# A decoder layer on one core: attention scores of a head on a 32-row tile, the router's columns beside the shared expert's, and a PE that is kept working ahead of the first product

## The reference

```python
# cross attention: 32 heads of 8 numbers, rotary positions on q and k
q = (x @ Wq).reshape(b, n, 32, 8);  k, v = split(ctx @ Wkv)
logits = einsum('bqhd,bkhd->bhqk', rope(q), rope(k)) / sqrt(8)
attn = einsum('bhqk,bkhd->bqhd', softmax(logits), v)
out = attn @ Wout + bout
# mixture of 8 experts (the best 2 by score), and a shared expert
scores = sigmoid(xt @ gate_w.T);  top_scores, sel = top_k(scores, 2)
h = silu(r @ w1[e].T) * (r @ w3[e].T);  out += h @ w2[e].T   # r = score * token
shared = silu(xt @ sw1.T) * (xt @ sw3.T) @ sw2.T
```

## Time and profile before

| | us |
|---|---|
| median of 3 runs | 674.62 (672.46 to 676.4) |
| profiled execution, its own time | 674.33 |
| its span in the trace | 672.4 |
| PE busy | 609.8 (91%) |
| DVE busy | 502.1 (75%) |
| ACT busy | 388.0 (58%) |
| POOL busy | 287.3 (43%) |

### The profile page before, as it was taken

How to read it: one execution, slowest core, us unless ns; L and a number is a source line. 1 busy time by engine, 2 the same in 40 slices (tenths; PEclk the granted TensorE clock), 3 DMA queues, 4 the chain that set the end, 5 groups by cost and what they waited for, 6 DMA issues and landing times. The chain is left out here.

```text
span 672.4 us, 14287 instructions
## 1 busy us (share of the span) xinstructions
PE 609.8 (91%) x4244; PEld 523.4 (78%) x4244; DVE 502.1 (75%) x1183; ACT 388.0 (58%) x1213; POOL 287.3 (43%) x326
## 2 busy tenths in 40 slices
PE   1887999999999999999999998646799999999998
PEld 1666888988888888888888888424578878878887
DVE  6884986987887888878869866824577867867756
ACT  2256557656756756665675666134576655656563
POOL 4353564654754754755646534356252112111000
PEclk9998999999999999999999999856989999999999
DMA  6000200200200200200202000161221211211100
GB/s 233 31 1 0 79 2 1 78 0 0 78 0 0 78 0 0 78 0 4 74 0 64 1 0 2 62 221 22 49 40 36 38 42 35 40 40 37 22 15 18
DMA packets 24142, 25.58 MB, mean 38 GB/s; under 512 B 3873, under 2 KB 19745, under 8 KB 23969
## 3 DMA queue, kind: packets, MB, share of 16 engines
q1 hardware_dynamic: 24096, 25.03, 13.1%
HBM read 17.55 MB, written 1.05 MB: 28 GB/s over the span
## 5 line engine op out<-in xcount | busy, mean ns | idle before, releaser
L797 POOL TENSOR_TENSOR sa_qe<-sa_ex,sa_enz 128x256 f32<-128x256 f32 x32 | 23.3, 728 | 85.6 <-ACT sa_ex L698 85.6
L724 ACT ACTIVATE sa_v<-bank 128x256 f32<-128x256 f32 x64 | 24.4, 382 | 59.2 <-PE bank L177 59.0
L175 PE MATMUL bank<-ht_hi,sa_qk_hi 128*128 128x512 f32 x128 | 55.4, 433 | 0.0
L175 PE MATMUL bank<-sa_vg_hi,ht_hi 128*128 128x512 f32 x128 | 52.6, 411 | 2.3 <-DVE sa_st L650 1.7
L698 ACT ACTIVATE sa_ex<-sa_okb,sa_minus_top 128x64 f32<-128x64 f32 x128 | 42.8, 339 | 17.0 <-DVE sa_minus_top L593 17.0
L791 POOL TENSOR_TENSOR sa_qt<-sa_rope_cos,sa_rope_sin 128x512 f32<-128x512 f32 x32 | 41.2, 1287 | 26.9 <-DVE sa_rope_sin L639 25.6
L637 DVE TENSOR_TENSOR sa_rope_cos<-bank,con 128x512 f32<-128x512 f32 x64 | 43.8, 684 | 9.6 <-PE bank L177 9.5
L177 PE MATMUL bank<-ht_hi,sa_qk_lo 128*128 128x512 f32 x128 | 50.7, 396 | 0.0
L177 PE MATMUL bank<-sa_vg_hi,ht_lo 128*128 128x512 f32 x128 | 50.6, 395 | 0.0
L176 PE MATMUL bank<-sa_vg_lo,ht_hi 128*128 128x512 f32 x128 | 50.5, 395 | 0.0
L176 PE MATMUL bank<-ht_lo,sa_qk_hi 128*128 128x512 f32 x128 | 50.4, 394 | 0.0
(11 more groups left out here) (215 smaller groups left out, 2018.4 us busy)
## 6 DMA issues: line engine op xcount, KB each, us to landing
sa_qk_raw<-in_wqk SPq DMA_DIRECT2D x8, 512.0 KB, 4.9
sa_vg_raw<-in_wvg SPq DMA_DIRECT2D x8, 512.0 KB, 3.3
xf_k_diag<-xf_kt SPq DMA_DIRECT2D x64, 48.0 KB
xf_q_diag<-xf_qt SPq DMA_DIRECT2D x64, 48.0 KB
sa_wo_raw<-in_wo SPq DMA_DIRECT2D x8, 256.0 KB, 3.5
xf_w_raw<-in_w SPq DMA_DIRECT2D x2, 640.0 KB, 10.0
xf_w_raw<-in_w SPq DMA_DIRECT2D x1, 1152.0 KB, 8.2
xs<-in_x SPq DMA_DIRECT2D x2, 512.0 KB, 4.6
```

What stands on the lines that cost most here:

```text
L175: pe.matmul(out, w_hi, m_hi, start=first, stop=False)
```

## The change

Eight things change, in the code and in the order tables.

1. The scores. `k_diag` and `q_diag` go, with their two clearings and 128 DMAs. `qt` has two buffers. A step L1 or L2 is now sixteen matmuls of 32 rows by 128 columns: head hl of a group lies on rows 32 hl of the array and writes into bank hl of four, j is the group. Two such steps per batch stand for eight of before; each takes four places of the ring of six at once (`parts_of`). The row of maxima goes into `qt` by four DMAs as before.
2. Since a bank now holds four groups of one hl, the maxima, the values' columns and the division are indexed the other way round (lines with `neg_top`, `col`, `DV`).
3. The router's 8 columns stand behind the shared expert's 256 in `w13_hi` and `w13_lo`; GT is one product of 264 columns that does U 0 too, and the step U 0 is gone. GT now runs in its batch's own turn.
4. All tables of `cross_ffn` are new, SP's steps KD and QD gone.
5. PE makes 22, 6 and 10 transposes of the constant identity into bank 7 in the head: before the first half of the turned input, between the halves, and behind them.
6. The product with `ws1` waits for the first half of `ht` alone, and for the second half ahead of its own.
7. POOL's `qk_lo` waits until all eight normalisations are done.
8. In turns -2 to 0 POOL's steps ROT and LO stand ahead of the WL steps.

```diff
-    def tensor(self, pe, normalised_here=True):
+    def tensor(self, pe, normalised_here=True, before=lambda half: None):
         for half in range(2):
+            before(half)
...
-            norm.tensor(pe)
-
-            pe.wait_ge(norm.hi_done, 4)
-            pe.wait_ge(norm.lo_done, 4)
+
+            def keep_clocked(turns_over):
+
+                for _ in range(turns_over):
+                    pe.transpose(banks[7][:, 0:TOK], ident, ident)
+
+            norm.tensor(pe, before=lambda half: keep_clocked((22, 6)[half]))
+            keep_clocked(10)
             pe.wait_ge(ws1_lo_done, 1)
             for half in range(2):
+                pe.wait_ge(norm.hi_done, 2 * half + 2)
+                pe.wait_ge(norm.lo_done, 2 * half + 2)
...
             norm.pool(pool)
+            pool.wait_ge(norm.hn_done, SEQS)
             pool.wait_ge(qk_hi_done, 1)
...
-X_PE = [("L2", 0), ("L2", 1), ("L2", 2), ("G", 0), ("L2", 3), ("U", 0), ("AV", 0), ("AV", 1), ("U", 1), ("L1", 0),
+X_PE = [("L2", 0), ("G", 0), ("AV", 0), ("AV", 1), ("T", 0), ("U", 1), ("AV", 2), ("AV", 3), ("L2", 1), ("U", 2),
...
+def parts_of(step, n):
+
+    return range(4 * n, 4 * n + 4) if step in ("L1", "L2") else (n,)
...
                     if step in FILLERS:
-                        ps = filled(step, n, b)
-                        wait_bank(pe, step, n, b)
+                        for part in parts_of(step, n):
+                            wait_bank(pe, step, part, b)
+                        ps = filled(step, parts_of(step, n)[0], b)
...
-                        pe.matmul(ps[:, :], qt[:, n, :], k_diag[:, n, :, :].rearrange("p h t -> p (h t)"),
-                                  start=True, stop=True).then_inc(pe_l1, 1)
+                        four = [filled(step, part, b) for part in parts_of(step, n)]
+                        for j in range(4):
+                            for hl in range(4):
+                                rows = slice(hl * QUAD, (hl + 1) * QUAD)
+                                mm = pe.matmul(four[hl][:, j * TOK:(j + 1) * TOK], qt[rows, b % 2, 4 * n + j, :],
+                                               kt[rows, p, 4 * n + j, :], start=True, stop=True)
+                                if j == 3:
+                                    mm.then_inc(pe_l1, 1)
...
-                            mm = split_product(pe, ps[:, 0:EXPERTS], ht_hi[:, kc, cols], ht_lo[:, kc, cols],
-                                               gate_hi[:, kc, :], gate_lo[:, kc, :], kc == 0, kc == KC - 1)
-                        mm.then_inc(pe_gt, 1)
+                            mm = split_product(pe, ps[:, 0:2 * HID + EXPERTS], ht_hi[:, kc, cols], ht_lo[:, kc, cols],
+                                               w13_hi[:, kc, both], w13_lo[:, kc, both], kc == 0, kc == KC - 1)
+                        mm.then_inc(pe_u, 1)
...
-                        if b == 0:
-                            dve.memset(k_diag[:, :, :, :].bitcast(F32), 0.0).then_inc(k_diag_set, 1)
...
-                            wait(act, pe_l1, done(b - 1, 7, 8))
-                            wait(act, q_diag_in[n - GT_QT], 64 * b)
-                            ins = act.activation(qt[:, 4 * (n - 5):4 * (n - 4), :], ps, ACT.Copy)
+                            wait(act, pe_l2, done(b - 2, 7, 8))
+                            ins = act.activation(qt[:, b % 2, 4 * (n - 5):4 * (n - 4), :], ps, ACT.Copy)
...
-                        if b == 0 and n == 1:
-                            pool.memset(q_diag[:, :, :, :].bitcast(F32), 0.0).then_inc(q_diag_set, 1)
```

More of the change, by code:

```diff
@@ L916, with w13_of @@
 RAW = 4
+W13_ALL = NE * 2 * HID + EXPERTS
+def w13_of(e):
+    first = (e - 1) % NE * 2 * HID
+    return slice(first, first + 2 * HID)
 TURNS = range(-2, SEQS + 1)
@@ L935, in steps_of @@
             yield step, n, b
+def parts_of(step, n):
+    return range(4 * n, 4 * n + 4) if step in ("L1", "L2") else (n,)
 def fill_places():
-    fills = [(step, n, b) for turn in TURNS for step, n, b in steps_of(PE_TABLES, turn) if step in FILLERS]
+    fills = [(step, part, b) for turn in TURNS for step, n, b in steps_of(PE_TABLES, turn) if step in FILLERS for part in parts_of(step, n)]
     return fills, {f: p for p, f in enumerate(fills)}
@@ L1143, in _ @@
                             pe.wait_ge(g_act, done(b, G_ACT[6], len(G_ACT)))
-                        if n % 4 == 0:
-                            pe.wait_ge(k_diag_in[n // 4], 64 * (b + 1))
-                        pe.matmul(ps[:, :], qt[:, n, :], k_diag[:, n, :, :].rearrange("p h t -> p (h t)"),
-                                  start=True, stop=True).then_inc(pe_l1, 1)
+                        four = [filled(step, part, b) for part in parts_of(step, n)]
[6 more added lines that the diff above has]
+                                    mm.then_inc(pe_l1, 1)
                     elif step == "L2":
-                        if n % 4 == 0:
-                            pe.wait_ge(q_diag_in[n // 4], 64 * (b + 1))
                         if n == 0:
                             pe.wait_ge(q_top_in, 64 * (b + 1))
-                        pe.matmul(ps[:, :], kt[:, p, n, :], q_diag[:, n, :, :].rearrange("p h t -> p (h t)"),
-                                  start=True, stop=True).then_inc(pe_l2, 1)
+                        four = [filled(step, part, b) for part in parts_of(step, n)]
+                        for j in range(4):
+                            for hl in range(4):
+                                rows = slice(hl * QUAD, (hl + 1) * QUAD)
+                                mm = pe.matmul(four[hl][:, j * TOK:(j + 1) * TOK], kt[rows, p, 4 * n + j, :],
+                                               qt[rows, b % 2, 4 * n + j, :], start=True, stop=True)
+                                if j == 3:
+                                    mm.then_inc(pe_l2, 1)
                     elif step == "AV":
@@ L1396, in _ @@
                     elif step == "GT":
-                        act.wait_ge(pe_gt, done(b))
+                        act.wait_ge(pe_u, done(b, 0, NE))
                         wait(act, routed, done(b - 1))
-                        act.activation(two_plus[:, :], filled(step, n, b)[:, 0:EXPERTS], ACT.Exp, scale=-1.0).then_inc(gate_exp_done, 1)
+                        act.activation(two_plus[:, :], filled(step, n, b)[:, 2 * HID:2 * HID + EXPERTS], ACT.Exp, scale=-1.0).then_inc(gate_exp_done, 1)
+                        if b == 0:
+                            act.wait_ge(half_set, 2)
+                        wait(act, gated_done, done(b, -2, NE))
+                        act.activation(th[:, NE * b % 2, :], filled(step, n, b)[:, 0:HID], ACT.Tanh, scale=half_scale[:, b, 0:1]).then_inc(th_done, 1)
                     elif step == "U":
@@ L1402, in _ @@
                         act.wait_ge(pe_u, done(b, n, NE))
-                        if b == 0 and n == 0:
-                            act.wait_ge(half_set, 2)
                         if n == 1:
```

101 lines of the change are left out of this document (40 added, 61 removed), and 68 rows, old and new, of tables (X_ACT, X_ACT_FIRST, X_ACT_LAST, X_DVE).

## The result

The changed kernel takes 656.07 us (median of 4 runs, 653.45 to 657.62) against 675.02 for the kernel before (4 runs on the same chip, 672.46 to 676.4). The ratio is 0.971 (95% interval 0.968 to 0.975), a gain of 19 us where 24 were forecast. The profiled execution took 655.79 us, its span 653.9 (before 674.33 and 672.4).

What follows compares the result with a forecast made beforehand. PE bounds the middle turns, chains of engines the head and first turns. 4.0 + 8.0 + 7.0 + 5.2 + 3.0 - 3.0 = 24.2 us off 674.33 gave 650, range 641 to 665.

Steps and rivals of the forecast that it cites:

- The sign: Whole kernel: faster by more than the 0.5% (3.4 us) by which two measurements can differ, chance 0.87.
- the likeliest case: Whole kernel: the forecast of 650 us, counted as 643 to 657, chance 0.71.
- Head, 4.0: Head: `qk_lo` held back and transposes lifting PE's clock gain 4.0 us, ends 1.5 and 6.
- The price of a slow stretch, 1.5: Head: PE idling longer ahead of SN lowers its clock, costing 3 us, half hidden: 1.5 where it happens.
- First turns, 8.0: First cross-attention turns: clearings and DMAs gone, ROT and LO earlier, gain 8.0 us, ends 3.5 and 10.5.
- Scores, 7.0: L1 and L2 in PE-bound turns: 26 new steps at 0.65 us replace 104 old at 0.23, gain 7.0 us.
- The sum of 0.85: Score step: by the skill's rule each of four rounds pays load and stream, 0.85 us a step, gain only 1.8.
- Router, 5.2: Router in eight batches: six matmuls of 0.67 us become eight columns more on others at 0.02, gain 5.2 us.
- Wait for the maxima, 3.0: L2's 1.04 us wait for TT's DMAs: of some 4 us in four turns, 3 gained.
- New waits, -3.0: Score steps take four of six banks at once: 0.12 us of waiting on each of 26 steps, cost 3.0 us.
- the ring as a bound (662): Middle turns: the ring of banks becomes the bound, they stay at 25.3 us, total 662, chance 0.16.
- Row tiles one after another (684): Score steps: row tiles do not run side by side, 1.8 us a step instead of 0.65, total 684, chance 0.08.

Runs made afterwards that it cites:

- the run of the head alone: The kernel before with only the three head edits (38 transposes, `ws1` product by halves, `qk_lo` behind the normalisations): 670.64 us, ratio 0.993.
- the router's columns apart: The changed kernel with the router's 8 columns again as six matmuls of their own, ahead of the shared expert's: 663.70 us, ratio 0.985.
- half a maximum: The changed kernel with DVE's maxima read over only the first half of the keys: 652.82 us, ratio 0.969.
- the middle table: The changed kernel with turn 6 run by the table of the middle turns instead of the last table: 656.72 us, ratio 0.973.
- the clock held up: The changed kernel with 111 more identity transposes in PE's gaps from the end of the slot attention to turn 0: 648.14 us, ratio 0.961.
- With the gaps filled: The changed kernel with all added transposes (111, 24, 14), turn 6 by the middle turns' table, `vg_lo` behind `us`'s last instruction: 642.94 us, ratio 0.954.

## Why the prediction was right, and where it was off

The sign, the likeliest case and the range held: 656 lies in 641 to 665, at the upper end of the forecast's own 643 to 657. That it came so near owes something to terms that were wrong in opposite ways. The terms one by one:

- **Head, 4.0.** Measured 3.7 at H in one trace against one, and 5 in the run of the head alone. The split was off: the wait of `qk_lo` carries two thirds, and the transposes, for which I put up to 2.2 us, bring about 1, because without the late normalisation PE's clock comes up nearly by itself. What I held against the full gain came true: `vg_lo` caught the copy of `us` (2.06 us), and PE's idle 3.31 us ahead of SN. The price of a slow stretch, 1.5, meets the measured 1.2 (4.9 at SN less 3.7 at H) by luck: I put it behind the gap ahead of SN, where in this trace the clock stayed up (SN's four matmuls in 0.66 us), and it was paid behind the gap near 54 us, which the kernel before had too. The Trainium skill, SBUF — State Buffer, section "Who interferes with whom", also says that a DVE instruction with two inputs in SBUF contends with GpSimd's reads. The runs agree: the last instruction of `us`, with both inputs in SBUF, took 2.94 us beside `vg_lo` and 0.75 without. I had read only its sentence on the copies, and so the version that holds `vg_lo` behind the copy missed.
- **First turns, 8.0.** Measured 7.9 at the L2 of batch 1, but from other parts, and between 5 and 10 by the other traces of the same code (43.6 to 48.4 us against 53.5). The clearings were mis-sized: 7.0 forecast, 3.7 measured for two of 3.04 and 3.08 us. At full length I estimate 4.7: POOL's 3.51, and 1.2 for DVE's, whose product for q started 5.96 us behind H before and 4.73 after; the rest of DVE's lies beside PE's product with `wq`. From H to the first L1 the gain is 9.8, so some 5 come from the transfers into `k_diag` and the order on POOL, for which I had 1.5; no run parts these two. Of the 10.3 at the first L2, 2.4 are gone by batch 1's, and there PE's clock counted: with it held up this stretch and the ones around it were 7.3 us shorter. I had seen the low clock in the earlier trace rows and took the chain to be the other engines'.
- **Scores, 7.0.** This is the step that failed in size. The distance of 0.60 us was right (0.6 to 0.7 forecast), and the four of a round start within 0.03 us. But I took 0.65 for the whole step, with 0.08 for the way in and the way out as held in AV's 0.57. Between plain products it costs 0.79: 0.09 in, and 0.10 in the product behind, the same 0.23 that the earlier trace rows show behind AV and that I wrote down and then did not add. Such an L2 saves 0.93 - 0.79 = 0.14 us, one behind AV 0.93 - 0.60 = 0.33, and an L1 nothing, as it is entered another 0.1 us later. With seven, seven and twelve of them this makes 3.3 us and not 7.0, most of the missing 5.3. On TensorE: Matmul & The Clock Gate, section "Part 3: Packing small matmuls — row/col tiling", of the Trainium skill: its speed-up of 3.07 for four row tiles, given there for 512 columns, agrees with the 3.2 measured here for 128 (1.93 to 0.60). The sum of 0.85 that I drew from its rule on loads lies nearer to what a step costs than mine, but for another reason: the rounds stand 0.10 us apart behind the first, and on one row tile the matmuls 0.12, so load and stream did not add up to 0.16.
- **Router, 5.2.** Borne out: 4.8 in the trace of the router's columns apart.
- **Wait for the maxima, 3.0.** More than borne out: 3.5 us of waits gone in turns 2 to 5, and 0.8 in turn 1.
- **New waits, -3.0.** The size was too small by about a third, and the place is not as I said. In turns 2 to 5 the list has no wait for a bank, only 0.8 for `hn`, and half a maximum changes nothing. They came where PE has little else to do. Turn 6 should have gained 0.5 from the scores and 0.5 from the router and lost 1.1, so 2.1 went to waits, as much as PE's idle time grew there (0.2 to 2.3); half a maximum or the middle table gives 0.7 to 0.9 of it back each. From the L2 of batch 1 to the end of turn 1 it took 29.0 us instead of 29.4, where 1.9 were due (scores 0.5, router 0.6, maxima 0.8), 1.5 less; PE's list has 1.1 for ACT's `wt` there, and with the clock held up the stretch took 28.1. I had not looked at turn 6 apart at all.

With the measured sizes the stretch from batch 1's L2 to the end comes to 3.3 + 4.0 (of the router) + 4.3 - 0.8 - 2.1 - 1.5 = 7.2 us, measured are 6.9. The last two terms are what turns 6 and 1 left over, so the sum is a test for the others alone: in turns 2 to 5 they make 0.47 + 0.54 + 0.87 - 0.20 = 1.7 us a turn, and 1.8 are measured. Why L1 is entered later stays open.

The rivals: the ring as a bound (662) did not come true in the middle. It holds for the second L1 of the program and, beside other waits, at the end; PE's list for 598 to 654 us has:

```profile
PE bank L1210 <- DVE xf_hid L1327: 1.2, 4, 0.7
...
PE bank L1141 <- DVE xf_neg_top L1255: 0.6, 1, 0.6
```

Row tiles one after another (684) was mis-priced: 1.93 us a step and 703 us. But the mechanism is as told, and four row groups are what keeps it away.

## What to carry to other kernels

A small-tile step costs its distance to the next start, plus what the first matmul behind it and the way into it lose; against four wide matmuls at 0.23 us these 0.2 us decide. Such steps are cheapest next to others that have paid for the way in or out, here L2 behind AV. Where a chain of engines is the bound and PE's clock is low in it, fill PE's gaps with harmless transposes and look again before writing that PE's speed is hidden: here that was worth about as much as the scores and the router together. If an instruction of DVE is freed from one of GpSimd's, see which comes next: hold the GpSimd instruction behind the last of the chain (done here only together with the transposes, where SN came at 20.56 instead of 21.76 us).

## What the runs showed of the hardware

The same kernel's executions differ in time as they differ in clock: those of the changed kernel took 653.45, 655.79, 656.35 and 657.62 us at mean granted clocks of 0.974, 0.969, 0.963 and 0.958. A gap of PE of 3.14 us at the same place of the same code was followed by 9.9 us at 0.50 in the changed kernel's trace and by none in that of the router's columns apart; the gap ahead of SN (3.31, 3.48 us) once by SN's four matmuls in 0.66 and once in 1.11 us. With the gaps filled, the mean clock was 1.00 and the six runs took 642.09 to 645.36.

A product whose operands are left in float32 (`wkv`, 512 columns) stands 0.43 us ahead of the next matmul in the middle turns before, one in fp32r of the same width 0.23.

The granted clock does not tell of the start of a program: the `ws1` product of the kernel before had its matmuls 0.41 us apart on average, about half speed, while the profile gives 1.00 for that stretch (the last but two of this row's numbers). There only the distances show it.

```profile
20.00:25.00 5.00, 5.00 (x15) 3.89 (x14) 3.35 (x5) 0.88 (x2) 3.08 (x2) 1.00 0.15 43
```
